# Last attention: q, k and v products from float32 to three fp32r products of halves

## The reference, cut to what matters

```python
h = _sln(hidden, w, ln_g, ln_b, Wg, bg, Wb, bb)      # layer norm, scaled and shifted by the condition
qkv = (h @ Wqkv.T + bqkv).reshape(B, N, num_heads, hd, 3)
...
energy = jnp.einsum('bhqd,bhkd->bhqk', q, k)
att = jax.nn.softmax(energy, axis=-1) / D ** 0.5
out = jnp.einsum('bhqk,bhkd->bhqd', att, v)
out = jnp.moveaxis(out, 1, 2).reshape(B, N, D)
out = out @ Wp.T + bp
h1 = out + hidden
h2 = _sln(h1, w, ln_g, ln_b, Wg, bg, Wb, bb)
return h2 + h1
```

## Time and profile before

| | |
|---|---|
| median of 3 runs | 873.48 us (872.41 to 874.89) |
| the profiled execution, first to last instruction | 872.2 us |
| TensorE busy | 829.4 us, 95% |
| VectorE busy | 680.4 us, 78% |
| ScalarE busy | 459.2 us, 53% |
| mean granted TensorE clock | 0.985 of full |

### The profile page before, as it was taken

One profiled execution on the slowest core, in us unless ns is written; L12 is line 12 of the kernel. 1 busy time (PEld: TensorE's weight loads), 2 busy tenths in 40 slices (PEclk: granted clock), 3 DMA queues, 4 the chain that ended last, 5 costly groups with the idle time before them and its releaser, 6 DMA issues.

```text
span 872.2 us, 13436 instructions
## 1 busy us (share of the span) xinstructions
PE 829.4 (95%) x5042; PEld 526.0 (60%) x5042; DVE 680.4 (78%) x1160; ACT 459.2 (53%) x840; POOL 227.2 (26%) x377
## 2 busy tenths in 40 slices
PE   5999999999999999999989989999999999999993
PEld 3667888988998998887835433343334333433342
DVE  7998667778558578647458979999999999999377
ACT  4746232143432443333232168878887888888760
POOL 4433512203003003112012620333333333333411
PEclk9999999999999999999989989999999999999998
DMA  8613132110000000000696600505050515000102
GB/s 310 260 50 98 49 99 99 49 53 1 1 1 1 2 1 1 1 1 1 183 212 152 255 1 3 94 21 93 21 94 21 93 22 99 23 25 21 27 25 73
DMA packets 29379, 57.40 MB, mean 66 GB/s; under 512 B 7228, under 2 KB 15152, under 8 KB 29314
## 3 DMA queue, kind: packets, MB, share of 16 engines
q1 hardware_dynamic: 22596, 44.40, 19.5%
q0 software_dynamic: 6720, 12.15, 4.8%
HBM read 39.26 MB, written 14.91 MB: 62 GB/s over the span
## 4 chain that ended last, share of the span: by engine, by line
PE 81%; DVE 11%; ACT 4%; issue 2%; DMA 1%; POOL 1%; SPq 0%; DVEq 0%; ACTq 0%
PE PA L1555 15%; PE PA L1566 14%; PE PD L1342 10%; PE PA L1320 8%; PE PD L1526 6%; PE PA L1431 5%; PE PD L1400 4%; PE PA L1268 3%; PE PA L1387 3%; PE PA L1261 2%; DVE NMX L2097 1%; PE PD L1624 1%; PE PA L1501 1%; PE PA L1421 1%; ACT R L1122 1%
## 5 line engine op out<-in xcount | busy, mean ns | idle before, releaser
L2097 DVE TENSOR_REDUCE NMX<-PD 128x2 f32<-128x1024 f32 x256 | 302.1, 1221 | 23.6 <-PE PD L1526 19.1
L1122 ACT ACTIVATE R<-PA 128x512 f32<-128x512 f32 x512 | 267.0, 603 | 70.2 <-PE PA L1555 68.5
L1555 PE MATMUL PA<-STKR 50*128 50x512 f32 x512 | 184.1, 450 | 3.8 <-ACT R L1122 2.7
L1555 PEld LDWEIGHTS PA<-STKR 50*128 50x128 f32 x512 | 82.3, 186 | 151.4 <-ACT R L1122 140.8
L1526 PE MATMUL PD<-STKR 48*128 48x512 f32 x512 | 148.4, 452 | 2.3 <-DVE NMX L2097 2.3
L1058 ACT ACTIVATE R<-PA,VEC 128x512 f32<-128x512 f32 x64 | 43.8, 687 | 104.1 <-PE PA L1320 91.6
L1342 PE MATMUL PD<-WHR,HSR 128*128 128x256 f32 x512 | 95.4, 286 | 0.5 <-DVE HSR L1942 0.5
L1342 PEld LDWEIGHTS PD<-WHR,HSR 128*128 128x128 f32 x512 | 82.1, 191 | 6.1 <-issue 2.0
L1320 PE MATMUL PA<-XSR,WHR 128*128 128x512 f32 x256 | 81.2, 398 | 3.8 <-issue 2.0
L1526 PEld LDWEIGHTS PD<-STKR 48*128 48x128 f32 x512 | 61.0, 186 | 28.1 <-DVE NMX L2097 13.8
L1941 DVE CAST HSR<-R 128x512 fp32r<-128x512 f32 x64 | 28.4, 444 | 57.8 <-ACT R L1058 57.8
(11 more groups left out here) (301 smaller groups left out, 1216.9 us busy)
## 6 DMA issues: line engine op xcount, KB each, us to landing
STKR<-qk_terms SPq DMA_DIRECT2D x32, 384.0 KB, 8.6
R<-in_l_w SPq DMA_DIRECT2D x8, 1024.0 KB, 5.1
W<-in_w SPq DMA_DIRECT2D x4, 1024.0 KB, 10.2
qk_terms<-PARTS SPq DMA_DIRECT2D x8, 512.0 KB, 3.7
qk_terms<-PARTS POOLq DMA_DIRECT2D x8, 512.0 KB, 3.4
S<-row_reciprocals POOLq DMA_DIRECT2D x56, 64.0 KB, 2.1
X<-in_x SPq DMA_DIRECT2D x4, 512.0 KB, 9.7
qk_terms<-PARTS SPq DMA_DIRECT2D x8, 256.0 KB, 4.6
```

The lines of the kernel that those rows point to most:

```text
L1122: act.activation(PB[:, n % 2, j, :], PA[:, e % NEB, :], ACT.Exp).then_inc(s_exp3, 1)
L1555: pe.matmul(PA[:, e % NEB, :], KS[rows, slot(gg), jj, kt * P:(kt + 1) * P], QS[rows, slot(gg), jj, c * HALF:(c + 1) * HALF], start=True, s ...
L2097: ve.tensor_reduce(out, PD[:, o:o + NROW, :], axis=AX_X, op=ALU.max, negate=True).then_inc(s_mred, 1)
```

## The change

The weights `WQ3` are split in place once, in a new stage `w3`: ScalarE rounds them to `WQH`, VectorE leaves the rest in `WQL` (which is `WQ3`'s own room). ScalarE writes each modulated half tile twice, as the high part and as float32 into `XT`, and VectorE subtracts to get the low part. `qk3` and `v3` then use three fp32r products per term: 6 matmuls for a q or k job in place of 2 float32 ones, 12 for a v job in place of 4. ScalarE copies the v results without a bias. The bias of v is turned (stage `bt`), multiplied by the output weights (`bm`), scaled and added to the output's bias row, for which GpSimd waits before its first use.

```diff
-SECOND = mlps(..., {NTILE: [("x2", 0)], ...
+SECOND = mlps(..., {NTILE - 3: [("w3", 0)], NTILE: [("x2", 0)], ...
-SCHED += [("x2", 1), ("qk3", 4), ("a1", 1), ("g", 1), ("qk3", 5), ("mx", 0), ("qk3", 6), ...
+SCHED += [("x2", 1), ("qk3", 4), ("a1", 1), ("bt", 0), ("g", 1), ("qk3", 5), ("mx", 0), ("bm", 0), ("qk3", 6), ...
...
+            WQH = at("WQH", C20 + T // 2, [P, 3, KB, D])
+            WQL = at("WQL", WA0 + 4 * KB * D, [P, 3, KB, D])
+            XH0 = at("XH0", C20 + 2 * T, [P, KB, T])
...
+        X3 = [[XH0[:, :, :], XTR[:, 0]], [XTR[:, 0], XTR[:, 1]]]
+        W3 = [WQH, WQL]
+        VB3 = DG[:, 0]
...
# GpSimd, first step
+                    po.wait_ge(s_bp3, 1)
...
# ScalarE
+            def last_weights(_):
+                act.wait_ge(s_w3in, 32)
+                act.wait_ge(s_sfull, B * NT)
+                act.activation(WQH[:, :, :, :], WQ3[:, :, :, :], ACT.Copy).then_inc(s_w3high, 1)
+
+            def last_tiles(b):
+                for job in turned(b, "n3"):
+                    _, _, h, k = job
+                    o, q = bank(*job), P3 * KB + k
+                    for dst in (X3[b][0], XT[:, b]):
+                        i = act.activation(dst[:, k, h * HALF:(h + 1) * HALF], o, ACT.Identity,
+                                           bias=PAR[:, b, q + KB:q + KB + 1], scale=PAR[:, b, q:q + 1])
+                    i.then_inc(s_aev, 1)
+
+            def v3(j):
+                ...
+                act.activation(VP[b][:, 2 * j:2 * j + 2, :, 0:HD],
+                               bank(b, "v3", j).rearrange("p (t h d) -> p t h d", t=2, h=HEADS), ACT.Copy).then_inc(s_aev, 1)
...
# TensorE, qk3
-                xt_ready(b, "n3", c)
-                project(abank(b, tag, side, c, k), WQ3[:, side], k * P, b, c, s_afull)
+                    pe.wait_ge(s_w3half, 1)
+                pe.wait_ge(s_half3, (b * NC + c + 1) * KB)
+                o = abank(b, tag, side, c, k)
+                terms = [(i, w, x) for i in range(KB) for w, x in TERMS]
+                for n, (i, w, x) in enumerate(terms):
+                    m = pe.matmul(o, W3[w][:, side, i, k * P:(k + 1) * P], X3[b][x][:, i, c * HALF:(c + 1) * HALF],
+                                  start=(n == 0), stop=(n == len(terms) - 1))
+                m.then_inc(s_afull, 1)
# TensorE, v3
-                    for k in range(KB):
-                        m = pe.matmul(o[:, u * D:(u + 1) * D], XT[:, b, k, t * P:(t + 1) * P], WQ3[:, 2, k, :],
-                                      start=(k == 0), stop=(k == KB - 1))
+                    for n, (k, w, x) in enumerate(terms):
+                        m = pe.matmul(o[:, u * D:(u + 1) * D], X3[b][x][:, k, t * P:(t + 1) * P], W3[w][:, 2, k, :],
+                                      start=(n == 0), stop=(n == len(terms) - 1))
...
+            def bias_turned(b):
+                o = abank(b, "bt")
+                for k in range(KB):
+                    m = pe.transpose(o[:, k * P:(k + 1) * P], BC[:, BV3, k * P:(k + 1) * P], ident[:, :])
+                m.then_inc(s_afull, 1)
+
+            def bias_projected(b):
+                evacuated(pe, b, "bt")
+                o = abank(b, "bm")
+                for k in range(KB):
+                    m = pe.matmul(o[:, 0:D], VB3[:, k, :], WP3[:, k, :], start=(k == 0), stop=(k == KB - 1))
+                m.then_inc(s_afull, 1)
...
# VectorE
-            def v3(j):
-                ...
+            def last_weights(_):
+                ve.wait_ge(s_w3high, 1)
+                ve.tensor_tensor(WQL[:, :, :, :], WQ3[:, :, :, :], WQH[:, :, :, :].bitcast(F32), ALU.subtract).then_inc(s_w3half, 1)
+
+            def last_halves(b):
+                for job in turned(b, "n3"):
+                    _, _, h, k = job
+                    high, low = (a[:, k, h * HALF:(h + 1) * HALF] for a in X3[b])
+                    evacuated(ve, *job)
+                    ve.tensor_tensor(low, XT[:, b, k, h * HALF:(h + 1) * HALF], high.bitcast(F32), ALU.subtract).then_inc(s_half3, 1)
+
+            def bias_turned(b):
+                ve.tensor_copy(VB3.rearrange("p k m -> p (k m)"), bank_of(b, "bt")[:, 0:KB * P]).then_inc(s_aevd, 1)
+
+            def bias_projected(b):
+                row = BC[:, BP3, :]
+                ve.scalar_tensor_tensor(row, bank_of(b, "bm")[:, 0:D], float(D) ** -0.5, row, ALU.mult, ALU.add).then_inc(s_aevd, 1)
+                evacuated(ve, b, "bm")
+                ve.sem_inc(s_bp3, 1)
```

More of the change, by code:

```diff
@@ L116 @@
 SECOND = mlps(1, "n2", {0: [None, ("pr", 1), ("pn", 1)]},
-              {NTILE: [("x2", 0)], NTILE + 1: [("a1", 0)], NTILE + 2: [("g", 0)], NTILE + 3: [("a2", 0)], NTILE + 4: [("f2", 0)],
+              {NTILE - 3: [("w3", 0)], NTILE: [("x2", 0)], NTILE + 1: [("a1", 0)], NTILE + 2: [("g", 0)], NTILE + 3: [("a2", 0)], NTILE + 4: [("f2", 0)],
                NTILE + 5: [("fn", 0)], NTILE + 7: [("n3", 0), ("qk3", 0), ("qk3", 1)],
@@ L121 @@
 SCHED = [x for x in SCHED if x]
-SCHED += [("x2", 1), ("qk3", 4), ("a1", 1), ("g", 1), ("qk3", 5), ("mx", 0), ("qk3", 6), ("mx", 1), ("a2", 1), ("mx", 2), ("mx", 3),
+SCHED += [("x2", 1), ("qk3", 4), ("a1", 1), ("bt", 0), ("g", 1), ("qk3", 5), ("mx", 0), ("bm", 0), ("qk3", 6), ("mx", 1), ("a2", 1), ("mx", 2), ("mx", 3),
           ("f2", 1), ("qk3", 7), ("mx", 4), ("v3", 0), ("mx", 5), ("v3", 1), ("fn", 1), ("mx", 6), ("v3", 2), ("mx", 7), ("v3", 3),
@@ L212, in act_jobs @@
         return [(b, "v3", j)]
-    if stage in ("a1", "a2"):
+    if stage in ("a1", "a2", "bt", "bm"):
         return [(b, stage)]
@@ L265, in evacuations @@
     for _, tag, *_ in jobs:
-        by_dve = int(tag in ("ad", "gc", "wt", "wv", "q", "k", "v1", "p", "o", "qk3", "v3", "f2"))
+        by_dve = int(tag in ("ad", "gc", "wt", "wv", "q", "k", "v1", "p", "o", "qk3", "f2", "bt", "bm"))
         seen[by_dve] += 1
@@ L428, in build @@
         SUMS, HN = S2[:, 0:HALF], S2[:, HALF:2 * HALF]
-        RS, RSR = C2[:, HALF:HALF + UNIT], C2[:, HALF + UNIT:HALF + 2 * UNIT]
+        RS, RSR = (C2[:, NPART * P + 32 + i * UNIT:NPART * P + 32 + (i + 1) * UNIT] for i in range(2))
+        X3 = [[XH0[:, :, :], XTR[:, 0]], [XTR[:, 0], XTR[:, 1]]]
+        W3 = [WQH, WQL]
+        VB3 = DG[:, 0]
         UOS = [UO[:, :], TG[:, :]]
@@ L523, in build @@
         s_hi = sem("qk_high_ready")
+        s_w3high = sem("last_attention_weights_high_ready")
+        s_w3half = sem("last_attention_weight_halves_ready")
+        s_half3 = sem("last_layer_tile_halves_ready")
+        s_bp3 = sem("last_bias_row_ready")
         s_ones = sem("ones_ready")
@@ L1045, in modulated @@
                 return f
+            def last_weights(_):
[11 more added lines that the diff above has]
+            def v3(j):
+                b, j = divmod(j, TWO)
+                if b == 0 and j == 0:
+                    act.wait_ge(s_dfull, DJ[(1, "w21", NT - 1)] + 1)
+                act.activation(VP[b][:, 2 * j:2 * j + 2, :, 0:HD],
+                               bank(b, "v3", j).rearrange("p (t h d) -> p t h d", t=2, h=HEADS), ACT.Copy).then_inc(s_aev, 1)
             def copied(stage, dst, func=ACT.Copy):
@@ L1128, in _ @@
                  "ma": modulated_tile("ma", PM, 0), "mb": modulated_tile("mb", PM, 0), "m": modulated_tile("m", PM, 0), "n1": modulated("n1", P1),
-                 "n2": modulated_tile("n2", P2, 1), "n3": modulated("n3", P3),
+                 "n2": modulated_tile("n2", P2, 1), "n3": last_tiles, "w3": last_weights, "v3": v3,
                  "u0": hidden("u0", ACT.Gelu_apprx_tanh, "b1", 0), "u1": hidden("u1", ACT.Gelu, "mb1", 1),
@@ L1497, in v3 @@
                 o = abank(b, "v3", j)
+                terms = [(k, w, x) for k in range(KB) for w, x in TERMS]
                 for u in range(2):
                     t = 2 * j + u
-                    for k in range(KB):
-                        m = pe.matmul(o[:, u * D:(u + 1) * D], XT[:, b, k, t * P:(t + 1) * P], WQ3[:, 2, k, :],
-                                      start=(k == 0), stop=(k == KB - 1))
+                    for n, (k, w, x) in enumerate(terms):
[12 more added lines that the diff above has]
+                    m = pe.matmul(o[:, 0:D], VB3[:, k, :], WP3[:, k, :], start=(k == 0), stop=(k == KB - 1))
                 m.then_inc(s_afull, 1)
@@ L1650, in _ @@
                  "a2": down("a2", lambda b: GT, 1, gelu_ready), "f2": f2,
-                 "n3": turn("n3", lambda b: XN[:, b], "f2"), "qk3": qk3, "v3": v3, "mx": maxpass, "tm": turn_max,
+                 "n3": turn("n3", lambda b: XN[:, b], "f2"), "qk3": qk3, "v3": v3, "bt": bias_turned, "bm": bias_projected, "mx": maxpass, "tm": turn_max,
                  "step": step, "hd": heads_turned, "hx": heads_back, "p3k": p3_ahead, "p3a": p3_first, "p3": p3})
@@ L2071, in qk3 @@
                                         ALU.subtract).then_inc(s_aevd, 1)
-            def v3(j):
-                b, j = divmod(j, TWO)
-                n = AJ[(b, "v3", j)]
-                if b == 0 and j == 0:
-                    ve.wait_ge(s_dfull, DJ[(1, "w21", NT - 1)] + 1)
```

(8 more changed lines are left out.)

2 lines of the change are left out of this document (1 added, 1 removed).

## The result

| | before | after |
|---|---|---|
| median of the runs | 873.37 us (872.41 to 874.89, 4 runs) | 878.51 us (876.42 to 879.38, 4 runs) |
| ratio, 95% interval | | 1.0056 [1.0039, 1.0073] |
| profiled execution | span 872.2, clock 0.985 | span 877.5, clock 0.977 |

The change made the kernel 0.56% slower. I had forecast 874.0 us, no measurable change, with a range to 877.5. What made it slower is what rival C had, a low clock for longer, but at another place than where I had put it. The profiled execution after is the slowest of its four (879.38 us), so the profile shows a little more low clock than the median execution has.

What follows compares the result with a forecast made beforehand. TensorE was taken as the bound, with VectorE close behind just ahead of the steps. The terms +4.6 - 0.7 + 1.2 - 1.8 - 2.8 = +0.5 us on 873.48 gave 874.0 us, range 870.0 to 877.5.

Steps and rivals of the forecast that it cites:

- rival C: At 474 to 493, the clock stays or falls low where VectorE sets the pace: slower, 876.9 us; chance 0.17.
- the steps: The 128 steps of the last attention, 504.8 to 845: not touched by the change, costed at nothing.
- signs of being wrong: First gap under 2 us, clock at 1.0 through both gaps, or the steps themselves changing length.
- My reckoning of what a fall costs: Half of the work in a half-clock stretch is lost: 1.7 us of 3.4 us at half.
- The first tile: Sequence 0, 410 to 417: TensorE waits +3.7 us for VectorE's subtraction, then a clock fall, +2.2 us.
- Rival B: Neither gap shows: VectorE reaches the subtractions sooner or the tile's other half feeds TensorE; 866.9 us, chance 0.06.
- rival A: Both gaps, ahead of jobs 0 and 8, are there but the clock does not fall; 870.6 us, chance 0.17.
- upper bound of +4.8: First tile's wait if each VectorE subtraction took 1.10 us, as one did beside a GpSimd addition.
- From 436 to 493: Job 8 starts earlier, -0.7; a second clock fall, +1.2; VectorE's waits for ScalarE go, -1.8.
- the fall of +1.2: Second clock fall, behind TensorE's 2.3 us wait ahead of job 8, slowing jobs 8 and 9; 0 to +1.5.
- The v jobs: At 493.2 to 504.8: -2.0 from shorter jobs, -0.8 behind the last one without VectorE's v additions; -2.8 us together.
- The weights: New stage w3 at 372 to 377: VectorE needs 1.9 us, covered by its idle time; costed at nothing.

Runs made afterwards that it cites:

- e14: Changed kernel with useless products filling both TensorE waits at the start of the steps (ahead of the last maximum pass, for the first Exp): 874.38 us.
- e16: Changed kernel with the waits ahead of job 0, ahead of the last maximum pass and for the first Exp all filled with useless products: 874.55 us.
- e9: Changed kernel with 15 useless products filling TensorE's 4.0 us wait ahead of job 0: 876.21 us.
- e4: Changed kernel with only q and k in halves; v is one float32 product of the high parts, its bias added by VectorE: 876.42 us.
- e1: Changed kernel with jobs 0 and 1 of q and k moved behind the next MLP tile: 872.17 us.
- e12: Changed kernel with jobs 0 and 1 moved, the exponential's table loaded early, and both waits at the first energies filled with useless products: 867.15 us.
- e10: Changed kernel with 7 useless products filling TensorE's wait for the first Exp: 878.8 us.
- e13: Changed kernel with four useless products filling TensorE's 1.09 us wait ahead of the last maximum pass: 878.9 us.
- e3: Changed kernel with only v in halves; q and k are one float32 product of the high parts: 874.73 us.
- e15: Changed kernel with useless products filling the second tile's waits ahead of jobs 8 and 9: 877.91 us.
- e11: Kernel before with 7 useless products behind the first three energies, in the wait for the first Exp: 874.58 us.

## Why the prediction was wrong

**The term that failed: the steps, costed at nothing.** I wrote of the 128 steps that "the change doesn't touch them". It adds no instruction to them, but their beginning runs at half clock for 13.7 us instead of 6.6, and costs 3.2 us; the end of the kernel gives 0.7 more, where the eight matmuls of the output projection take 3.00 us instead of 1.97. These 3.9 us are most of the 4.8 by which the two profiled executions differ from my sum. That the steps would change length was one of the signs of being wrong that I had named.

What low clock costs there is read from the profiles where ScalarE's table is loaded late, as in both kernels. The stage takes 23.9 us with no low clock (e14, e16), 25.4 to 25.6 with 6.6, 26.9 to 27.0 with 10.2, 28.5 to 28.6 with 13.7 and 29.9 with 17.3 (e9). In the kernel before the low stretch begins at 505.2, so that TensorE's wait of 1.77 us for the first Exp (to 507.10) lies in it and only 4.8 us of it are work; in the kernel after it begins at 509.2, behind that wait. So it cost 1.5 us for 4.8 before and 4.7 for 13.7 after, 0.31 and 0.34 for each us of work at half clock. My reckoning of what a fall costs (half of the work that it falls on) came near at the first tile, where 3.4 us at half clock cost 1.5 and not 1.7, and was too high for the steps, where TensorE also waits for ScalarE between its matmuls; that these waits take up the difference is argued and not shown. I only counted falls up to 474 and put the rival for more of them, C, at 474 to 493, where the clock stayed at 1.00. The kernel before already had a fall behind its first energies, which no row of mine showed: I had looked for low clock in the stretches that the change edits, and took 0.99 over 340 us for full.

The runs as a whole go with this. In 118 of 119 executions of the kernel before (one of 885.1 us is left out), the span grows by 0.40 us for each us of low clock (2 x (1 - clock) x span). The medians are 24.4 us low before and 36.8 after, and 12.4 x 0.40 = 5.0 us: about the whole of the difference. This is an estimate, since an execution that waited longer somewhere can also have more low clock for it. The table gives the same from the two profiles: the clock has 1.5 us at the first tile, 3.2 at the first energies and 0.7 at the end, together 5.4 where the spans differ by 5.3. At equal clock the change would thus be worth about nothing, its wait eating what its shorter products save.

**The first tile: right in its wait, near in its fall.** The gap was predicted at 3.7 us more and came at 3.75 (4.03 against 0.28), released by VectorE's subtraction behind the four additions, as described. The fall behind it was there and cost 1.5 us instead of 2.2: it was 3.4 us long in this execution, and little but jobs 0 and 1 lay in it. In the profiles of e4 and e14, with the same wait, it is 6.8 us long, so my 2.2 lies between the two lengths. With the 1.3 us of shorter jobs the stage gives +4.0 instead of +4.6. Rival B falls, and so does A at this place. My upper bound of +4.8 was mis-added: two subtractions of 1.10 behind 414.82 end at 417.02, +4.5; nothing rests on it. The four subtractions took 2.48 us, 0.62 each, and not 1.10. The Trainium skill (SBUF — State Buffer, SBUF: two separate sides) would have them locked out only beside a GpSimd instruction that reads there, and by that rule the trace agrees: the last GpSimd addition ahead of them ends at 413.69, the subtractions start at 414.13. The fall and its absence with a filled wait (granted clock 0.72 and 1.00 over 415.5 to 421.5) also bear out what the Trainium skill (TensorE: Matmul & The Clock Gate, Part 1) has as the default, a throttled engine that activity releases.

**From 436 to 493: half right.** Predicted -0.7, +1.2 and -1.8, together -1.3; measured -0.5. Job 8's wait was 2.29 us as said (2.3), but no fall followed it: the granted clock is 1.00 from 475.9 on, so here it went as rival A had it. In its place job 9 waited 0.58 us for the other half of the tile. And VectorE kept two waits for ScalarE, 1.2 us together, where I had all four of them go, and a woven job takes 1.60 and not 1.39, which leaves less room; that this is the reason is argued and not shown. That the stretch from job 8 to the v jobs came out near my sum (-0.8 against -0.6) is luck: the fall of +1.2 did not come, and of the -1.8 only 0.8 came.

**The v jobs: mis-sized.** Predicted -2.8, measured -1.45. The 1.92 us of a v job in the earlier trace rows stood between two passes, and the 1.43 that I set against it stood in a row of like matmuls. Woven, twelve matmuls take 1.63 (and six of q or k 1.60, against 1.37 back to back in e1). So the saving was 0.29 a job and not 0.49, and the pitch is 2.05 us and not 1.86. Of the -0.8 behind the last job 0.2 came: TensorE's last wait went from 1.33 to 1.09 us. In the kernel after VectorE stands idle for 0.83 us and starts its reduction at 504.46, 0.54 us behind the start of the pass at 503.92; in the kernel before, behind its additions, it starts at 503.02, 0.78 behind the pass at 502.24. So the additions had cost it only 0.24 us.

**The weights: right.** ScalarE's copy took 1.48 us and VectorE's subtraction 1.76 (predicted 1.9), from 372.69 on; VectorE still has its idle time, 9.34 us ahead of 394.66 (9.35 in the earlier trace rows), and TensorE's part up to the first tile is no longer (409.72 against 410.34).

**What stays open.** Shown is that the low stretch at the first energies goes when both waits there are filled (e14, e16, e12), and stays when one is (e10, e13). Not shown is why it is 13.7 us in the changed kernel and 6.6 in the one before, whose waits there are as long (1.33 and 1.77, against 1.09 and 1.79). A part of it may be the execution that was profiled: the changed kernel's versions with both waits left as they are have 13.7 (the kernel after, e1), 17.3 (e9), 10.2 (e4), 6.7 (e3) and 6.6 us (e15), and the kernel before with one wait filled has 10.3 (e11). The long form was not seen with v alone in halves (e3), which points to the load ahead of it, but filling the largest wait further back left the median where it was (e15). So the clock's part of the loss is measured, and what ties its length to this change is not.

## What to carry to other kernels

When a change lightens TensorE or makes it wait, look up the granted clock at the beginning of the next dense stage too, even where the change has no instruction: a low stretch there is charged to work that was never touched, here at 0.3 to 0.4 us for each us. A product that is shorter by a fifth (1.37 against 1.72 us) was worth nothing here while the engine that prepares its operands came to them behind other work; look first for a place one tile further back for the consumer (two lines of the order, 6.3 us here). Take the price of an operation that is woven with others from woven rows, of old and new alike. And where the clock falls, look at more than one execution before a fall is put down to an edit.

## What the runs showed of the hardware

- Behind one and the same wait of 4.03 us the clock fell at different times. In the kernel after TensorE restarted at 415.66 at full rate (0.23 us a matmul), and the matmuls became slow (0.43 us apart) from 417.20 on, 1.5 us into the work; in e14 the granted clock fell at about 414.3, inside the wait and 1.5 us ahead of the restart at 415.82. The low stretch was 3.4 us long in the one and 6.8 in the other.
- Behind two waits of 1.1 and 1.8 us, with 1.0 us of work between them, 13.7 us of half clock followed. With either of them filled by useless products the stretch was as long (13.7), and with both filled it was gone. A wait of 2.29 us elsewhere was followed by no fall.
- Six matmuls of 512 columns take 1.57 to 1.60 us where they stand between groups of another shape, and 1.37 in a row of like ones.
- A single late transfer of row sums (2.98 us of waiting for VectorE) cost one execution 5.4 us, with 10.3 us of low clock behind it. Over 118 executions of the kernel before, more low clock goes with a longer span at 0.40 us for each us.
